# Feed-forward of a transformer pair: three of eight back products in half-precision terms, with the back products three steps behind

## The chip, the cores and the metric

The kernel runs on one core of one Trainium2 chip. The metric is the device time of one execution in microseconds. PE is the matrix engine (TensorE), DVE, ACT and POOL are VectorE, ScalarE and GpSimd; SP issues most transfers.

## What is computed

Two transformer layers on x of 4 x 1024 tokens of 256 values: cross-attention, a mixture of experts, a second cross-attention, and last a low-rank feed-forward, each on the normalised rows and added to x. The change is in the last one:

```
P = x_normalised @ U1            # 256 -> 64
H = gelu(P @ V1 + b1)            # 64 -> 1024, tanh form
Q = H @ U2                       # 1024 -> 64
x = x + Q @ V2 + b2              # 64 -> 256
```

All inputs and the output are single precision.

## The kernel before

Stages follow one another: preparation, first attention, routing, a stage that runs the experts and then the second attention (`experts_and_attend`), and `feed_forward` (from L2189). The feed-forward works in eight units of 512 tokens (UNITS). A unit's 1024 hidden values are eight steps m of 128 (MS); j counts steps over all units. Every engine has its own instruction list, written out by hand in loops, and the lists meet in semaphores.

The steps of a unit, with the names of the program:
- `unit_rows` (L2114) and `unit_normed` (L2131) on DVE and `unit_deviation` (L2124) on POOL normalise a row tile of 128 tokens: statistics (L2117, L2119), variance plus epsilon (L2121), the power -0.5 on POOL (L2128), and the normalised row (L2136). POOL also adds b2 to the row of x (`biased`, L2231). The same functions serve the first four row tiles at the end of the second attention.
- `rows_transposed` (L2249, four transposes into x_ps) on PE, copied out by ACT (L2315).
- `low_rank` (L2256): x times U1 into 64 rows for each half of the unit, one half on column half 0 to 63 of the array, the other on 64 to 127. ACT takes its high half in half precision (`high`, L2321), DVE the low rest (`low`, L2351).
- `first(u, m)` (L2269): six half-precision products on row halves of the array (three terms, two halves), into one of two banks h_ps.
- `gelu(u, m)` on ACT (L2327): h_ps to h in single precision, four buffers.
- `back(u, m)` (L2279): h times U2, single precision, two products on the two column halves, accumulated over m in low2_ps.
- `second` (L2356) copies low2_ps to SBUF, PE's `result` (L2288) multiplies by V2, DVE's `result` (L2364) adds x, SP stores.

On PE the order of a unit is first 0, first 1, the result of the unit before, then back m and first m + 2 in turn, the low rank of the next unit, and backs 6 and 7. A first waits until the gelu two steps earlier has read its bank; a back waits for its gelu. In the second attention DVE's `sums` and `heads` (L2024, L2031) feed PE's L1696; `expand` (L2042, L2044), which splits V1 into half-precision terms, stands in DVE's list there, in the step k = QUARTERS - 4.

```
for m in range(6):
    back(u, m)
    first(u, m + 2)
    if more and m in (1, 4):
        rows_transposed(2 * u + 2 + m // 4)
```

Of the kernel before, what the change touches and what calls it, by code (L numbers as in the profile page):

```python
# [31 lines left out]
P = 128  # L32
# [1254 lines left out]
def experts_and_attend(nc, A, G):  # L1287
# [3 lines left out]
    with ExitStack() as ctx:  # L1291
# [79 lines left out]
        with nc.Block() as block:  # L1371
# [538 lines left out]
            def _(dve):  # L1910
# [135 lines left out]

                for c in range(SOON, CHUNKS):
                    weights(c)
# [18 lines left out]
                for k in STEPS:  # L2067
# [22 lines left out]
                    if k == QUARTERS - 4:  # L2090
                        expand()
                    if QUARTERS - 3 <= k <= QUARTERS:
                        unit_rows(nc, dve, G, k - QUARTERS + 3)
# [20 lines left out]
def unit_rows(nc, dve, G, n):  # L2114
# [3 lines left out]
    dve.wait_ge(f.ch, 2 * n + 1)  # L2118
    nc.vector.bn_aggr(f.mv[:, i, :], f.stats[:, i, :]).then_inc(f.ch, 1)  # L2119
    dve.wait_ge(f.ch, 2 * n + 2)  # L2120
    nc.vector.tensor_scalar(f.ve[:, i, :], f.mv[:, i, 1:2], EPS, None, ALU.add).then_inc(f.var_ok, 1)  # L2121


def unit_deviation(nc, pool, G, n):  # L2124

    f = G["f"]
    pool.wait_ge(f.var_ok, n + 1)
    nc.gpsimd.tensor_tensor(f.rstd[:, n % 4, :], f.ve[:, n % 4, :], G["neghalf"][:, :], ALU.pow).then_inc(f.rstd_ok, 1)  # L2128


def unit_normed(nc, dve, G, n):  # L2131

    f = G["f"]
    dve.wait_ge(f.rstd_ok, n + 1)
# [28 lines left out]
def allocate_last(nc, ctx, G):  # L2163
# [15 lines left out]
    G["b1"], G["w2"], G["b2"] = Q.sb("b1_f", [P, HID // P]), Q.sb("v2_f", [2 * RANK, D]), Q.sb("b2_f", [P, D])  # L2179
    G["ff_in"] = L.sem("ff_in")  # L2180
# [8 lines left out]
def feed_forward(nc, A, G):  # L2189
# [3 lines left out]
    UNITS, U, MS = NT // 4, 4 * P, HID // P  # L2193
    with ExitStack() as ctx:
# [5 lines left out]
        h = Q.sb("h_f", [P, 4, U])  # L2200
# [7 lines left out]
        b2_ok = L.sem("b2_ok_f")  # L2208
# [4 lines left out]
        u1, w1, w1h, b1, u2, w2, b2 = (G[n] for n in ("u1", "w1", "w1h", "b1", "u2", "w2", "b2"))  # L2213

        with nc.Block() as block:  # L2215
# [24 lines left out]
            def _(pe):  # L2240
# [19 lines left out]
                def first(u, m):  # L2260
                    j = u * MS + m
                    if m == 0:
                        pe.wait_ge(llo_ok, u + 1)
                        if u == 0:
                            pe.wait_ge(w1h_ok, 2)
# [7 lines left out]
                def back(u, m):  # L2273
                    j = u * MS + m
                    pe.wait_ge(h_ok, j + 1)
                    if m == 0:
                        after(pe, low2_ok, u)
                    for i in range(2):
                        last = mm(low2_ps[flat(i, RANK), :], u2[:, m, :], h[:, j % 4, flat(i, U // 2)],  # L2279
                                  start=m == 0, stop=m == MS - 1)  # L2280
# [12 lines left out]
                for u in range(UNITS):  # L2293
                    more = u + 1 < UNITS
                    first(u, 0)
                    first(u, 1)
                    if u:
                        result(u - 1)
                    for m in range(6):
                        back(u, m)  # L2300
                        first(u, m + 2)
                        if more and m in (1, 4):
                            rows_transposed(2 * u + 2 + m // 4)
# [118 lines left out]
```

## Time and profile before

| | |
|---|---|
| median of 3 runs | 997.5 us (995.8 to 999.16) |
| the profiled execution | 1003.9 us |
| its span in the trace | 1001.9 us |
| PE busy | 918.6 us, 92% of the span |
| DVE, ACT, POOL busy | 616.3, 513.4, 422.1 us |
| TensorE clock granted, mean | 0.97 of full |

The span runs from the first to the last instruction of the trace; the profiled execution's time has 2.0 us more around it. Shares over the whole span mix stages with different limits, so a stage has to be read by itself: the feed-forward lies at the end, from about 903 us on.

### The profile page before, as it was taken

The numbers are of one execution on the slowest core, as the hardware profiler recorded it, in microseconds if no ns is written. First come the engines' busy times: TensorE is split into PE (matmuls) and PEld (weight loads), VectorE is DVE, ScalarE is ACT, GpSimd is POOL, SyncE is SP. The second block draws the span as 40 slices with busy tenths as digits, with TensorE's granted clock in tenths as the row PEclk, the third lists the DMA queues.
The fourth block names the chain that finished last, engine by engine and source line by source line (L and its number), as shares of the span: only waits on it lengthen the run. The fifth ranks groups of instructions, "written<-read, shape, count | busy, mean of one in ns | idle before, by whom it ended". The sixth has DMA issues, their size and how long they took to land. (4 is left out here: it accounts for less than half of the span.)

```text
span 1001.9 us, 23945 instructions
## 1 busy us (share of the span) xinstructions
PE 918.6 (92%) x8022; PEld 640.7 (64%) x8022; DVE 616.3 (62%) x1517; ACT 513.4 (51%) x873; POOL 422.1 (42%) x573
## 2 busy tenths in 40 slices
PE   6799999997458999999999999999989999889995
PEld 4555656554226788898898888888734444454552
DVE  3577888885787434454554545677468888545661
ACT  1478888886352433333333333333456767645663
POOL 2387777772201122334333224553176665204450
PEclk9999999999876999999999999999989999999998
DMA  6423444424541112111111212232143221000112
GB/s 178 89 65 106 114 145 117 141 88 151 154 160 43 44 44 59 43 43 54 54 43 48 60 44 67 90 90 68 33 113 91 81 78 39 2 1 15 51 46 61
DMA packets 73731, 75.46 MB, mean 75 GB/s; under 512 B 22730, under 2 KB 66874, under 8 KB 73626
## 3 DMA queue, kind: packets, MB, share of 16 engines
q1 hardware_dynamic: 67146, 56.31, 18.8%
q0 software_dynamic: 6480, 17.70, 6.7%
q8 instruction: 72, 1.18, 0.5%
q14 instruction: 33, 0.27, 0.1%
HBM read 51.64 MB, written 22.34 MB: 74 GB/s over the span
## 5 line engine op out<-in xcount | busy, mean ns | idle before, releaser
L1925 DVE CAST hh_e<-h_e 128x512 f16<-128x512 f32 x128 | 57.7, 451 | 151.6 <-ACT h_e L1800 87.7
L1564 PE MATMUL banks_ea<-xT_e,experts 128*128 128x256 f16 x512 | 139.6, 273 | 0.0
L1579 PE MATMUL banks_ea<-experts,hh_e 128*128 x512 | 139.6, 273 | 0.0
L1566 PE MATMUL banks_ea<-xT_e,experts 128*128 128x256 f16 x512 | 139.6, 273 | 0.0
L1580 PE MATMUL banks_ea<-experts,hh_e 128*128 x512 | 139.6, 273 | 0.0
L1565 PE MATMUL banks_ea<-xT_e,experts 128*128 128x256 f16 x512 | 139.6, 273 | 0.0
L1578 PE MATMUL banks_ea<-experts,hh_e 128*128 x512 | 139.6, 273 | 0.0
L1800 ACT ACTIVATE h_e<-banks_ea 128x512 f32<-128x512 f32 x128 | 76.4, 597 | 87.3 <-PE banks_ea L1566 87.3
L1383 POOL DMA_INDIRECT x_e<-xh_scratch,token x33 | 36.8, 1114 | 151.5 <-PE banks_ea L1505 105.5
L1927 DVE TENSOR_TENSOR hh_e<-h_e,hh_e 128x512 f16<-128x512 f32 x128 | 88.6, 692 | 4.4
L1854 ACT ACTIVATE experts<-banks_ea 77x1024 f32<-77x1024 f32 x64 | 64.8, 1014 | 41.0 <-PE banks_ea L1673 41.0
L625 POOL TENSOR_TENSOR experts<-keys,blocks 128x616 f16<-128x616 f16 x64 | 76.5, 1216 | 0.0
L1408 POOL DMA_INDIRECT w_late<-y_scratch,slots_t x64 | 62.5, 977 | 30.7 <-issue 16.7
L2010 DVE TENSOR_REDUCE lx<-banks_ea 128x4 f32<-128x308 f32 x128 | 60.3, 471 | 18.5 <-PE banks_ea L1644 18.0
L835 ACT ACTIVATE experts<-sT_ps 77x1024 f32<-77x1024 f32 x64 | 65.1, 1016 | 7.3 <-PE sT_ps L694 4.2
L1790 ACT ACTIVATE xT_e<-banks_ea 128x512 f16<-128x512 f32 (+1 forms) x39 | 21.8, 558 | 91.3 <-PE banks_ea L1505 91.3
L1380 POOL COPY idx_e<-token 128x2 int32 x19 | 11.6, 611 | 119.1 <-PE banks_ea L1505 119.1
L2327 ACT ACTIVATE experts<-h_ps_f,experts 128x512 f32<-128x512 f32 x64 | 43.2, 688 | 30.2 <-PE h_ps_f L2269 30.2
L928 DVE TENSOR_REDUCE qcat<-s_ps 128x8 f16<-128x616 f32 x64 | 51.0, 798 | 8.5 <-PE s_ps L720 4.3
L1817 ACT ACTIVATE y_e<-banks_ea 128x256 f32<-128x256 f32 x64 | 21.1, 381 | 67.0 <-PE banks_ea L1580 67.0
L1579 PEld LDWEIGHTS banks_ea<-experts,hh_e 128*128 128x128 f16 x512 | 50.0, 98 | 6.2
L1565 PEld LDWEIGHTS banks_ea<-xT_e,experts 128*128 x512 | 50.0, 98 | 6.2
(376 smaller groups left out, 2193.8 us busy)
## 6 DMA issues: line engine op xcount, KB each, us to landing
experts<-in_L_ffn_w SPq DMA_DIRECT2D x22, 512.0 KB, 4.0
y_scratch<-y_e SPq DMA_DIRECT2D x32, 256.0 KB, 3.3
x<-in_x SPq DMA_DIRECT2D x32, 128.0 KB, 3.2
experts<-in_x SPq DMA_DIRECT2D x64, 64.0 KB, 2.4
x_scratch<-x SPq DMA_DIRECT2D x16, 256.0 KB, 2.5
xh_scratch<-xn SPq DMA_DIRECT2D x16, 256.0 KB, 2.7
w_late<-in_L_ffn_w SPq DMA_DIRECT2D x8, 512.0 KB, 4.6
w_late<-x_scratch SPq DMA_DIRECT2D x32, 128.0 KB, 2.6
```

The lines of the kernel that those rows point to most:

```text
L625: nc.gpsimd.tensor_tensor(bd[:, f % 2, flat(i, 2), :, :], G["khi"][0][:, b, heads].rearrange("p (q k) -> p q k", q=2)[:, :, None, :] .broa ...
L835: nc.scalar.activation(prob[:, k % 2, qh, :, :], sT_ps[0:KEYS, :, :], ACT.Exp).then_inc(exp_ok, 1)
L1408: pool.indirect_dma_start(out=rows[:, f % 4, :], out_offset=None, in_=A["y"][0:EARLY_ROWS, :] if f < TB else A["y"], in_offset=bass.Indire ...
L1564: mm(out, w[0], xT[0][:, c, :], start=c == 0, stop=False)
L1565: mm(out, w[0], xT[1][:, c, :], start=False, stop=False)
L1566: last = mm(out, w[1], xT[0][:, c, :], start=False, stop=c == DC - 1)
L1578: mm(out, a[0], w[0], start=m == 0, stop=False)
L1579: mm(out, a[0], w[1], start=False, stop=False)
L1580: last = mm(out, a[1], w[0], start=False, stop=m == 7)
L1800: nc.scalar.activation(h[:, q % 2, :], up_ps[q], ACT.Gelu, scale=1 / WSCALE).then_inc(gelu_ok, 1)
L1854: nc.scalar.activation(prob[:, k % 2, 2 * half:2 * half + 2, :], sT_ps[0:KEYS, 2 * half:2 * half + 2, :], ACT.Exp, scale=1.0 / 16).then_in ...
L1927: nc.vector.tensor_tensor(hh[1][own], h[own], hh[0][own], ALU.subtract).then_inc(hlo_ok, 1)
```

## The change

In steps m = 1, 3 and 5 of every unit (SPLITS, 24 in all) the back product is made of half-precision terms. ACT runs the gelu a second time on the same bank, into half precision (hh, part 0). DVE subtracts it from the single-precision gelu (`split`, hh, part 1). U2 is multiplied by 64 and split in the same way into u2h (`expand_back`, after `expand`), and the back is three terms: high by high, high by low, low by high. The other five backs use the scaled U2 in single precision, and `second` divides by 64.

The backs trail the firsts by three steps (LAG) through all units without a break; the buffers of h become six (RING). The result of a unit moves behind first 3 of the next, low rank to step 6, the transposes to steps 2 and 4. DVE's list is rearranged, and its variance add (L2121) moves to POOL.

```diff
+                def expand_back():
+                    nc.vector.tensor_scalar(G["u2"][:, :, :], G["u2"][:, :, :], WSCALE, None, ALU.mult).then_inc(unit.w1h_ok, 1)
+                    dve.wait_ge(unit.w1h_ok, 3)
+                    nc.vector.tensor_copy(G["u2h"][:, 0, :, :], G["u2"][:, :, :]).then_inc(unit.w1h_ok, 1)
+                    dve.wait_ge(unit.w1h_ok, 4)
+                    nc.vector.tensor_tensor(G["u2h"][:, 1, :, :], G["u2"][:, :, :], G["u2h"][:, 0, :, :],
+                                            ALU.subtract).then_inc(unit.w1h_ok, 1)
...
                     if k == QUARTERS - 4:
                         expand()
+                        expand_back()
...
     nc.vector.bn_stats(f.stats[:, i, :], G["X"](n)).then_inc(f.ch, 1)
-    dve.wait_ge(f.ch, 2 * n + 1)
-    nc.vector.bn_aggr(f.mv[:, i, :], f.stats[:, i, :]).then_inc(f.ch, 1)
-    dve.wait_ge(f.ch, 2 * n + 2)
-    nc.vector.tensor_scalar(f.ve[:, i, :], f.mv[:, i, 1:2], EPS, None, ALU.add).then_inc(f.var_ok, 1)
+    dve.wait_ge(f.ch, n + 1)
+    nc.vector.bn_aggr(f.mv[:, i, :], f.stats[:, i, :]).then_inc(f.var_ok, 1)
...
     pool.wait_ge(f.var_ok, n + 1)
+    nc.gpsimd.tensor_scalar(f.ve[:, n % 4, :], f.mv[:, n % 4, 1:2], EPS, None, ALU.add).then_inc(f.rstd_ok, 1)
+    pool.wait_ge(f.rstd_ok, 2 * n + 1)
     nc.gpsimd.tensor_tensor(f.rstd[:, n % 4, :], f.ve[:, n % 4, :], G["neghalf"][:, :], ALU.pow).then_inc(f.rstd_ok, 1)
...
-    UNITS, U, MS = NT // 4, 4 * P, HID // P
+    UNITS, U, MS, RING, LAG = NT // 4, 4 * P, HID // P, 6, 3
+    SPLITS = [(u, m) for u in range(UNITS) for m in (1, 3, 5)]
...
-        h = Q.sb("h_f", [P, 4, U])
+        h, hh = Q.sb("h_f", [P, RING, U]), Q.sb("hh_f", [P, 4, 2, U], F16)
...
-                            pe.wait_ge(w1h_ok, 2)
+                            pe.wait_ge(w1h_ok, 5)
                     after(pe, h_ok, j - 1)
...
                 def back(u, m):
                     j = u * MS + m
-                    pe.wait_ge(h_ok, j + 1)
                     if m == 0:
                         after(pe, low2_ok, u)
-                    for i in range(2):
-                        last = mm(low2_ps[flat(i, RANK), :], u2[:, m, :], h[:, j % 4, flat(i, U // 2)],
-                                  start=m == 0, stop=m == MS - 1)
+                    if (u, m) in SPLITS:
+                        n = SPLITS.index((u, m))
+                        pe.wait_ge(split_ok, n + 1)
+                        for weight, part in ((0, 0), (0, 1), (1, 0)):
+                            for i in range(2):
+                                last = mm(low2_ps[flat(i, RANK), :], u2h[:, weight, m, :], hh[:, n % 4, part, flat(i, U // 2)],
+                                          start=m == weight == part == 0, stop=m == MS - 1 and weight == 1)
+                    else:
+                        pe.wait_ge(h_ok, j + 1)
+                        for i in range(2):
+                            last = mm(low2_ps[flat(i, RANK), :], u2[:, m, :], h[:, j % RING, flat(i, U // 2)],
+                                      start=m == 0, stop=m == MS - 1)
                     last.then_inc(back_done, 1)
...
                 low_rank(0)
-                for u in range(UNITS):
-                    more = u + 1 < UNITS
-                    first(u, 0)
-                    first(u, 1)
-                    if u:
+                for j in range(UNITS * MS + LAG):
+                    u, m = j // MS, j % MS
+                    if u < UNITS:
+                        first(u, m)
+                    if u and m == LAG and u < UNITS:
                         result(u - 1)
-                    for m in range(6):
-                        back(u, m)
-                        first(u, m + 2)
-                        if more and m in (1, 4):
-                            rows_transposed(2 * u + 2 + m // 4)
-                    if more:
+                    if u + 1 < UNITS and m == 6:
                         low_rank(u + 1)
-                    back(u, 6)
-                    back(u, 7)
+                    if j >= LAG:
+                        back((j - LAG) // MS, (j - LAG) % MS)
+                    if u + 1 < UNITS and m in (2, 4):
+                        rows_transposed(2 * u + 1 + m // 2)
                 result(UNITS - 1)
...
                 def gelu(u, m):
                     j = u * MS + m
                     act.wait_ge(h_done, j + 1)
-                    after(act, back_done, j - 3)
-                    nc.scalar.activation(h[:, j % 4, :].rearrange("p (i t) -> p i t", i=2), h_ps[j % 2], ACT.Gelu_apprx_tanh,
-                                         bias=b1[:, m:m + 1], scale=1 / WSCALE).then_inc(h_ok, 1)
+                    after(act, back_done, j - RING + 1)
+                    first = nc.scalar.activation(h[:, j % RING, :].rearrange("p (i t) -> p i t", i=2), h_ps[j % 2],
+                                                 ACT.Gelu_apprx_tanh, bias=b1[:, m:m + 1], scale=1 / WSCALE)
+                    if (u, m) not in SPLITS:
+                        first.then_inc(h_ok, 1)
+                        return
+                    n = SPLITS.index((u, m))
+                    if n >= 4:
+                        before = SPLITS[n - 4]
+                        act.wait_ge(back_done, before[0] * MS + before[1] + 1)
+                    nc.scalar.activation(hh[:, n % 4, 0, :].rearrange("p (i t) -> p i t", i=2), h_ps[j % 2],
+                                         ACT.Gelu_apprx_tanh, bias=b1[:, m:m + 1], scale=1 / WSCALE).then_inc(h_ok, 1)
 
                 high(0)
                 for u in range(UNITS):
                     more = u + 1 < UNITS
                     for m in range(MS):
                         gelu(u, m)
-                        if more and m in (3, 6):
-                            rows(2 * u + 2 + m // 6)
-                    if more:
-                        high(u + 1)
+                        if more and m in (2, 4):
+                            rows(2 * u + 1 + m // 2)
+                        if more and m == 6:
+                            high(u + 1)
...
-                    nc.vector.tensor_copy(low2[:, :], low2_ps).then_inc(low2_ok, 1)
+                    nc.vector.tensor_scalar(low2[:, :], low2_ps, 1 / WSCALE, None, ALU.mult).then_inc(low2_ok, 1)
+
+                def split(u, m):
+                    j = u * MS + m
+                    n = SPLITS.index((u, m))
+                    dve.wait_ge(h_ok, j + 1)
+                    if n >= 4:
+                        before = SPLITS[n - 4]
+                        dve.wait_ge(back_done, before[0] * MS + before[1] + 1)
+                    nc.vector.tensor_tensor(hh[:, n % 4, 1, :], h[:, j % RING, :], hh[:, n % 4, 0, :],
+                                            ALU.subtract).then_inc(split_ok, 1)
...
+                def next_row(n):
+                    if n < NT:
+                        if n + 1 < NT:
+                            rows(n + 1)
+                        normed_rows(n)
+
                 rows(4)
                 low(0)
+                next_row(4)
+                next_row(5)
                 for u in range(UNITS):
+                    if u == 0:
+                        next_row(6)
+                    next_row(4 * u + 7)
+                    if u:
+                        second(u - 1)
+                    split(u, 1)
+                    if u:
+                        result(u - 1)
+                    next_row(4 * u + 8)
+                    split(u, 3)
+                    next_row(4 * u + 9)
+                    split(u, 5)
                     if u + 1 < UNITS:
-                        for n in range(4 * u + 4, 4 * u + 8):
-                            if n + 1 < NT:
-                                rows(n + 1)
-                            normed_rows(n)
-                            if u and n % 4 == 2:
-                                result(u - 1)
                         low(u + 1)
-                    elif u:
-                        result(u - 1)
-                    second(u)
+                    next_row(4 * u + 10)
+                second(UNITS - 1)
                 result(UNITS - 1)
```

The order on PE around the border of two units, before. x_ps with 64x256 is the low rank, with 128x128 the transposes; h_ps is the first product, low_ps the back product, out_ps the result.

```order
L2269 MATMUL h_ps_f<-experts 128x256 x6
L2256 MATMUL x_ps_f<-experts 64x256 x4
L2279 MATMUL low_ps_f<-experts 64x256 x4
L2269 MATMUL h_ps_f<-experts 128x256 x12
L2288 MATMUL out_ps_f<-experts 128x256 x4
L2279 MATMUL low_ps_f<-experts 64x256 x2
```

The same border in the changed kernel, from the back product of step 3 to the result; L2294 is a split back, L2299 one in single precision.

```order
L2294 MATMUL low_ps_f<-experts 64x256 x6
L2281 MATMUL h_ps_f<-experts 128x256 x6
L2299 MATMUL low_ps_f<-experts 64x256 x2
L2281 MATMUL h_ps_f<-experts 128x256 x6
L2294 MATMUL low_ps_f<-experts 64x256 x6
L2281 MATMUL h_ps_f<-experts 128x256 x6
L2299 MATMUL low_ps_f<-experts 64x256 x2
L2281 MATMUL h_ps_f<-experts 128x256 x6
L2299 MATMUL low_ps_f<-experts 64x256 x2
L2261 MATMUL x_ps_f<-const,experts 128x128 x4
L2281 MATMUL h_ps_f<-experts 128x256 x6
L2308 MATMUL out_ps_f<-experts 128x256 x4
```

Two firsts or two backs no longer stand side by side, and three backs of a unit come after firsts of the next.

DVE's list at the end of the second attention, before:

```order
L2037 TENSOR_TENSOR experts<-banks_ea,experts 128x256
L2042 TENSOR_SCALAR experts<-experts 128x1024
L2044 SCALAR_TENSOR_TENSOR experts<-experts 128x1024
L2024 RECIPROCAL experts<-banks_ea 128x16
L2031 TENSOR_TENSOR experts<-banks_ea,experts 128x256
```

and in the changed kernel:

```order
L2037 TENSOR_TENSOR experts<-banks_ea,experts 128x256
L2042 TENSOR_SCALAR experts<-experts 128x1024
L2044 SCALAR_TENSOR_TENSOR experts<-experts 128x1024
L2049 TENSOR_SCALAR experts<-experts 128x512
L2051 CAST experts<-experts 128x512
L2053 TENSOR_TENSOR experts<-experts 128x512
L2024 RECIPROCAL experts<-banks_ea 128x16
L2031 TENSOR_TENSOR experts<-banks_ea,experts 128x256
```

The three instructions of `expand_back` stand ahead of the `sums` and `heads` of the same step.

DVE's list in unit 0, from the normalised row 6 on, before (L2351 is the low half of unit 1):

```order
L2136 TENSOR_SCALAR experts<-const,experts 128x256
L2117 BN_STATS experts<-experts 128x6
L2119 BN_AGGR experts<-experts 128x2
L2121 TENSOR_SCALAR experts<-experts 128x1
L2136 TENSOR_SCALAR experts<-const,experts 128x256
L2351 TENSOR_TENSOR experts<-x_ps_f,experts 128x256
```

and in the changed kernel (L2391 is `split`):

```order
L2146 TENSOR_SCALAR experts<-const,experts 128x256
L2127 BN_STATS experts<-experts 128x6
L2129 BN_AGGR experts<-experts 128x2
L2146 TENSOR_SCALAR experts<-const,experts 128x256
L2391 TENSOR_TENSOR experts<-experts 128x512
```

The first split stands behind row 7, and the low half of unit 1 behind the third split.

## Rows read from the trace of the kernel before

**Rows 1.** Stretches: length; busy of PE, PEld (weight loads), DVE, ACT, POOL; clock; DMA.

```profile
940.00:952.00 12.00, 11.92 (x120) 5.96 (x116) 7.42 (x25) 7.45 (x12) 6.30 (x11) 1.00 0.17 48
```

**Rows 2.** Timeline of PE, one unit: start, length, engine, line, operation.

```profile
937.59 0.83 PE L2269 MATMUL h_ps_f<-experts 64*128 64x256 f16 x12
938.25 1.03 PE L2288 MATMUL out_ps_f<-experts 64*128 64x256 f32 x8
939.21 0.65 PE L2279 MATMUL low_ps_f<-experts 128*64 128x256 f32 x4
939.79 0.50 PE L2269 MATMUL h_ps_f<-experts 64*128 64x256 f16 x6
940.23 0.65 PE L2279 MATMUL low_ps_f<-experts 128*64 128x256 f32 x4
...
947.40 1.03 PE L2279 MATMUL low_ps_f<-experts 128*64 128x256 f32 x8
948.51 0.83 PE L2269 MATMUL h_ps_f<-experts 64*128 64x256 f16 x12
```

**Rows 3.** Timeline, end of the second attention; in brackets idle time and its releaser.

```profile
873.59 1.22 DVE L2044 SCALAR_TENSOR_TENSOR experts<-experts 128x1024 f16<-128x1024 f32 x1
...
875.49 0.44 PE L1696 MATMUL banks_ea<-const,experts 128*128 128x128 f32 x2 [1.38 <-DVE experts L2031]
...
876.84 2.06 PE L1704 MATMUL banks_ea<-woT,experts 128*128 128x256 f32 x4
```

**Rows 4.** Timelines of PE and its weight loads: experts, and one feed-forward load.

```profile
500.06 0.27 PE L1566 MATMUL banks_ea<-xT_e,experts 128*128 128x256 f16 x1
500.17 0.27 PE L1578 MATMUL banks_ea<-experts,hh_e 128*128 x1
...
500.17 0.10 PEld L1579 LDWEIGHTS banks_ea<-experts,hh_e 128*128 128x128 f16 x1
...
936.90 0.14 PEld L2279 LDWEIGHTS low_ps_f<-experts 128*64 128x64 f32 x2
```

**Rows 5.** Timeline of PE in the first attention: half-precision products of three shapes.

```profile
203.07 0.28 PE L703 MATMUL t_ps<-ident,experts 128*128 128x128 f16 x2
203.27 0.33 PE L715 MATMUL s_ps<-experts 64*32 64x308 f16 x8
203.53 0.30 PE L720 MATMUL s_ps<-late,early 5*128 5x308 bf16 x2
```

**Rows 6.** Groups by line: busy us, mean ns of one, idle us before.

```profile
L2327 ACT ACTIVATE experts<-h_ps_f,experts 128x512 f32<-128x512 f32 x64 | 43.2, 688 | 30.2 <-PE h_ps_f L2269 30.2
...
L1927 DVE TENSOR_TENSOR hh_e<-h_e,hh_e 128x512 f16<-128x512 f32 x128 | 88.6, 692 | 4.4
...
L1925 DVE CAST hh_e<-h_e 128x512 f16<-128x512 f32 x128 | 57.7, 451 | 151.6 <-ACT h_e L1800 87.7 <-PE banks_ea L1580 59.9 <-PE banks_ea L1545 3.8
...
L2136 DVE TENSOR_SCALAR experts<-experts 128x256 f32<-128x256 f32 x24 | 12.3, 513 | 0.0
...
L2121 DVE TENSOR_SCALAR experts<-experts 128x1 f32<-128x1 f32 x32 | 4.9, 154 | 1.1
...
L2128 POOL TENSOR_TENSOR experts<-experts,neghalf 128x1 f32<-128x1 f32 x32 | 20.0, 625 | 77.0 <-DVE experts L2121 77.0
...
L2231 POOL TENSOR_TENSOR experts<-experts 128x256 f32<-128x256 f32 x24 | 17.3, 724 | 0.0
...
L639 POOL TENSOR_SCALAR ve<-mv 128x1 f32<-128x1 f32 x32 | 7.7, 240 | 39.5 <-DVE mv L922 39.5
```

**Rows 7.** Timeline of PE, the first products of units 0 and 1.

```profile
905.14 0.83 PE L2269 MATMUL h_ps_f<-experts 64*128 64x256 f16 x12 [0.94 <-DVE experts L2351]
...
915.73 0.83 PE L2269 MATMUL h_ps_f<-experts 64*128 64x256 f16 x12
```

**Rows 8.** Timeline of PE, the last back product.

```profile
989.88 0.65 PE L2279 MATMUL low_ps_f<-experts 128*64 128x256 f32 x4 [0.20 <-ACT experts L2327]
```

**Rows 9.** Table of stretches for PE: busy us, instructions, clock, DMA share, GB/s.

```profile
878.00:880.00 2.00, 2.00 (x11) 0.50 0.00 0
```

More of the change, by code:

```diff
@@ L2133, in unit_normed @@
     f = G["f"]
-    dve.wait_ge(f.rstd_ok, n + 1)
+    dve.wait_ge(f.rstd_ok, 2 * n + 2)
     after(dve, f.t_done, (n - 4) // 2 + 1)
@@ L2179, in allocate_last @@
     G["b1"], G["w2"], G["b2"] = Q.sb("b1_f", [P, HID // P]), Q.sb("v2_f", [2 * RANK, D]), Q.sb("b2_f", [P, D])
+    G["u2h"] = Q.sb("u2h_f", [P, 2, HID // P, RANK], F16)
     G["ff_in"] = L.sem("ff_in")
@@ L2207, in feed_forward @@
         xh_ok, t_done, xhT_ok, w1h_ok = f.xh_ok, f.t_done, f.xhT_ok, f.w1h_ok
-        b2_ok = L.sem("b2_ok_f")
+        b2_ok, split_ok = L.sem("b2_ok_f"), L.sem("split_ok_f")
         low_done, lhi_ok, llo_ok, h_done, h_ok, back_done, low2_ok, out_done, out_ok = (
@@ L2212, in feed_forward @@
         ident = G["const"][:, CC["ident"][0]:CC["ident"][1]]
-        u1, w1, w1h, b1, u2, w2, b2 = (G[n] for n in ("u1", "w1", "w1h", "b1", "u2", "w2", "b2"))
+        u1, w1, w1h, b1, u2, u2h, w2, b2 = (G[n] for n in ("u1", "w1", "w1h", "b1", "u2", "u2h", "w2", "b2"))
         with nc.Block() as block:
```

## Prediction

> **What bounds the kernel now.** I read the table of stretches first: in the middle of the feed-forward PE is busy 11.92 of 12.00 us, ACT 7.45, DVE 7.42, POOL 6.30 [rows 1]. PE sets the pace there and the others have a third to spare. The timeline of PE then shows one unit of 512 tokens [rows 2]: from the pair of first products at 937.59 to the next such pair at 948.51 is 10.92 us, each row starts before the one ahead of it ends, and none carries a wait. From start to start a back product takes 0.58 (939.21 to 939.79), a first product 0.44 (939.79 to 940.23), two adjacent firsts 0.66, the last two backs 1.11 with a short wait for the low halves in it. A unit changes by what these times add up to.
>
> The end of the attention, where the change adds three DVE instructions, is another matter. There PE waited 1.38 us for DVE's L2031 at 875.49, right after the expansion of the first weights (L2044 at 873.59) [rows 3]. What DVE gets to do at that place is paid in full.
>
> **Part 1: the split backs.** In 24 backs (three of eight in each of eight units) two single-precision products become six half-precision ones, on the same two column halves of the array. No row has half precision in this tile shape, so I bound it.
> - Streaming: in the expert stage a half-precision product of 256 columns starts every 0.11 us (500.06, 500.17) [rows 4]. Three pairs side by side are 0.33, which is also half of the 0.66 of two firsts.
> - Are the column halves side by side? In the first attention eight half-precision products of 308 columns, on 64 rows by 32 columns each, go from 203.27 to 203.53 [rows 5]. One by one, at the rate above, they would take 1.06, in row pairs alone 0.53. Column tiles run together in half precision.
> - The change of tile shape: a first costs 0.33 where the result product follows (half of 0.66) and 0.44 where a back follows. The result is single precision like the back, so the 0.10 belongs to the shape and not to the type. From half-precision transposes on 128 rows (two of 128 columns, 0.11 of streaming) to products on 64 rows it took 0.20 (203.07 to 203.27) [rows 5]: 0.09 again. If the eight products above all ran at once, 0.13 of their 0.26 was streaming and 0.13 overhead.
> - Weight loads: six instead of four. Two single-precision loads for the column halves lay within 0.14 at 936.90, and in the experts a load of 0.10 stands beside every product of 0.11 on the same rows [rows 4]. So I count none. The Trainium skill, "TensorE: Matmul & The Clock Gate", Part 3, The mechanism, states that a weight load overlaps products in flight only when the row groups differ. The halves share all rows; by that rule three pairs of loads of 0.10 would stand alone, a split would take 0.73, and the sum below would be +7.7 instead of +0.5. The expert products would then be 0.21 apart, and the trace has 0.11.
>
> I take 0.33 + 0.10 = 0.43 against 0.58: 0.15 saved in each. The ends are 0.33 (the shape costs nothing) and 0.46 (an overhead of 0.13).
>
> **Part 2: the new order on PE.** Result, low rank and transposes stay as many. Before, a unit held 0.66 (two firsts) + 6 x 0.58 + 6 x 0.44 + 1.11 = 7.89. Now firsts and backs alternate all the way: seven firsts at 0.44, one at 0.33 ahead of the result, five backs at 0.58, three splits at 0.43: 3.08 + 0.33 + 2.90 + 1.29 = 7.60. That is 0.29 less a unit. Some 0.2 of what the splits save is given back, because firsts and backs no longer stand in pairs. Units 1 to 6 give **-1.8 us**.
>
> **Part 3: cover on ACT, DVE and POOL.** The shares of rows 1 are, for one unit of 10.92, ACT 6.8, DVE 6.8, POOL 5.7. ACT gets three gelus at 0.69: 8.9. DVE gets three subtracts of 128x512, 0.69 by the same form in the experts, and loses four adds of 0.15: 8.2. POOL gets four adds of 0.24: 6.7 [rows 6]. All stay below the 10.6 of PE, so they cost nothing there. A split is ready some 2 us after its first product, its back comes three steps, 3 to 4 us, after it. The tightest place is the low half for the next unit, which stands behind the third subtract on DVE and ahead of the next unit's first product, with about 0.2 us of room; what it is late would be paid in seven units.
>
> **Part 4: unit 0.** It lasted 10.59 us (905.14 to 915.73) [rows 7]. Three backs slide into the next unit (-1.74), two of its own are split (-0.30). Against that, DVE now normalises rows 4 to 7 ahead of the first subtract, and POOL paces them: add 0.24, power 0.62, bias 0.72, so 1.58 a row [rows 6]. From some 0.5 us after the first product it needs 0.86 for row 5 and 2 x 1.58 for rows 6 and 7; with row 7 itself (0.51) and the subtract (0.69) the second back can start near 5.7. PE is there near 4.1 and stands 1.6 us. The third first product and the first transposes wait some 0.6 longer than PE waited here before. -2.04 + 2.2 = **+0.2**.
>
> **Part 5: the last unit.** It also does three backs of the unit before, 0.43 + 2 x 0.58 = 1.59. It saves 3 x 0.15 in its own splits, its last back no longer waits 0.20 for the last gelu [rows 8], and its last four backs stand together, two changes of shape less (0.2). **+0.8.**
>
> **Part 6: the end of the attention.** Scaling, cast and subtract of the second weights, 128x512 each, are 0.45 + 0.45 + 0.69 = 1.59 by the casts and subtracts of the experts [rows 6], and they stand between L2044 and the L2031 that PE waits for. Nothing hides them. Of the four adds of the variance (0.15 each) that leave DVE here I count two: the first falls where PE is busy, and for the last row DVE waits for POOL, which now does the add. **+1.3**. The ends: 0, if the steps after it take it up, and 2.3 by the clock. After the old wait the granted clock was 0.50 (878 to 880) [rows 9], the 1.2 GHz level, and L1704 took 2.06 at 876.84 [rows 3], half of which would do at full clock. A longer wait could bring one more such piece, 1.0 us, into the slow stretch.
>
> **Sum.** -1.8 + 0.2 + 0.8 + 1.3 = **+0.5 us**. The profiled execution took 1003.9 (span 1001.9, 2.0 around it) and would come to 1004.4. It lies 6.4 above the median of three runs, 997.5, so on that median the forecast is **998.0**. A measurement of this kernel tells about 0.3%, 3 us, from no change: I forecast no change.
>
> **Rivals.**
> - *The halves do not stream together* (slower). Six products in a line, 0.65 + 0.10 = 0.75 a split: 24 x 0.32 = +7.7 more, time 1005.7. For it: no half precision in just this shape. Against: rows 5. It decides from a split of 0.53 on, where the sum passes +3. Chance 0.05.
> - *Weight loads stand alone* (slower). 24 x 0.30 = +7.2, time 1005.2. For it: all six products of a split use all 128 rows. Against: both loads of rows 4. Chance 0.04.
> - *The shape costs nothing between half-precision products* (faster). First and split 0.33 each: 24 x 0.20 = -4.8, time 993.2. Against: the 0.20 of rows 5, with half precision on both sides. Chance 0.08.
> - *The clock falls once more*, in unit 0 where PE stands, or for longer in the attention. A slow stretch like that of rows 9 costs 1.0 to 1.7: time 999.0 to 999.7, beyond 3 us only with another miss. Chance 0.12.
> - *The change does not do what it says, because ACT or DVE takes over.* They would have to lose 2 us a unit to waits; one us beyond that is +7, time 1005. Against: part 3. Chance 0.05.
>
> The forecast has the rest, 0.66, spread over 994 to 1002 by the ends of part 1 (24 x 0.03 = 0.7 up), those of part 6, and the spread of runs (995.8 to 999.16); 0.08 of it lies beyond 3 us on either side. Faster: 0.08 + 0.08 = 0.16. Slower: 0.05 + 0.04 + 0.05 + 0.08, and 0.04 from the clock, 0.26. The same: 0.58. The range goes from the cheap shape (993.2, nearly) to the clock at its worst with the spread of runs: 993.5 to 1002.0.
>
> **What would show it.** Right: six products of a split in 0.42 to 0.46 from start to start, units of 10.6 us without a wait on PE, one wait of 1 to 2 us for DVE's subtract in unit 0, and a wait for L2031 near 2.9 instead of 1.38. Wrong: a split of 0.53 or more (part 1), firsts that wait for gelus or low halves in steady units (part 3), a wait for L2031 as before (part 6), or a granted clock of 0.50 within the feed-forward.

## The result, and the profile after

| | before | after |
|---|---|---|
| median | 997.53 us (994.53 to 1003.49) | 1000.7 us (998.14 to 1020.47) |
| ratio of the times | | 1.0033, 95% interval 1.0016 to 1.0049 |
| profiled execution, its span | 1003.9, 1001.9 | 1005.88, 1004.1 |
| PE, DVE, ACT, POOL busy | 918.6, 616.3, 513.4, 422.1 | 916.7, 631.9, 526.3, 434.1 |

The medians are of 20 runs each; the run of 1020.47 us, at a granted clock of 0.92, is left out of the ratio, as single runs far off are below. The changed kernel is 3.3 us slower (1.6 to 4.9). The forecast was no change, +0.5 us; the time lies within its range. Both profiled executions lie above their medians. Both also ran some 7 us at the lower clock from about 737 us on, ahead of everything that the change touches (granted clock 0.62 and 0.53 from 736 to 744 before, 0.56 and 0.59 after); in the profiles of other executions, further down, this stretch is there or not.

The steady units of the feed-forward did what they were meant to. The table of stretches of the changed kernel, columns as in [rows 1], shows PE busy without a gap; DVE and ACT have grown, and stay below PE:

```profile
940.00:952.00 12.00, 12.00 (x130) 6.18 (x126) 9.25 (x23) 9.30 (x16) 7.98 (x15) 1.00 0.20 55
```

PE's timeline of one unit, which answers to [rows 2]; L2281 is a first product, L2294 a split back, L2299 a back in single precision, L2308 the result:

```profile
943.53 1.03 PE L2308 MATMUL out_ps_f<-experts 64*128 64x256 f32 x8
944.49 0.65 PE L2299 MATMUL low_ps_f<-experts 128*64 128x256 f32 x4
945.07 0.50 PE L2281 MATMUL h_ps_f<-experts 64*128 64x256 f16 x6
945.51 0.52 PE L2294 MATMUL low_ps_f<-experts 128*64 128x256 f16 x6
945.96 0.66 PE L2261 MATMUL x_ps_f<-const,experts 128*128 128x128 f32 x4
...
954.19 1.03 PE L2308 MATMUL out_ps_f<-experts 64*128 64x256 f32 x8
```

The split back takes 0.45 from start to start (945.51 to 945.96), the single one 0.58 (944.49 to 945.07), and no row carries a wait. The next result starts at 954.19, so a unit lasts 10.66 instead of 10.92.

At the end of the attention DVE, and PE behind it (both in the timeline, for [rows 3]):

```profile
873.07 1.23 DVE L2044 SCALAR_TENSOR_TENSOR experts<-experts 128x1024 f16<-128x1024 f32 x1
...
874.21 0.42 DVE L2049 TENSOR_SCALAR experts<-experts 128x512 f32<-128x512 f32 x1
874.67 0.43 DVE L2051 CAST experts<-experts 128x512 f16<-128x512 f32 x1
875.13 0.69 DVE L2053 TENSOR_TENSOR experts<-experts 128x512 f16<-128x512 f32 x1
875.74 0.25 DVE L2024 RECIPROCAL experts<-banks_ea 128x16 f32<-128x16 f32 x1
876.02 0.42 DVE L2031 TENSOR_TENSOR experts<-banks_ea,experts 128x256 f32<-128x256 f32 x1
...
876.50 0.69 PE L1696 MATMUL banks_ea<-const,experts 128*128 128x128 f32 x2 [2.91 <-DVE experts L2031]
...
878.96 2.08 PE L1704 MATMUL banks_ea<-woT,experts 128*128 128x256 f32 x4
...
883.49 0.44 PE L1696 MATMUL banks_ea<-const,experts 128*128 128x128 f32 x2
```

PE's wait for L2031 grew from 1.38 to 2.91. The next round, from L1696 to L1696, took 6.99 (876.50 to 883.49); before it took 5.47 (875.49 to 880.96). The stretches say why: the clock stays at its lower level (0.50, 1.2 GHz) for about twice as long as before (PE first, then PEld, DVE, ACT, POOL, clock). The changed kernel:

```profile
876.00:878.00 2.00, 1.50 (x10) 0.45 (x10) 0.42 (x1) 0.38 (x1) 0.00 (x0) 0.60 0.00 0
878.00:880.00 2.00, 2.00 (x11) 0.86 (x4) 0.00 (x0) 0.91 (x2) 0.00 (x0) 0.50 0.00 0
880.00:882.00 2.00, 2.00 (x11) 1.38 (x13) 0.90 (x4) 0.60 (x1) 0.00 (x0) 0.50 0.00 0
882.00:884.00 2.00, 2.00 (x22) 0.75 (x22) 0.61 (x3) 0.40 (x1) 0.81 (x2) 0.69 0.00 0
```

and the kernel before, on either side of the stretch of [rows 9], with the start of its next round:

```profile
876.00:878.00 2.00, 2.00 (x11) 0.98 (x4) 0.00 (x0) 1.37 (x3) 0.00 (x0) 0.72 0.00 0
...
880.00:882.00 2.00, 2.00 (x26) 0.65 (x18) 0.70 (x3) 0.93 (x2) 0.55 (x1) 0.92 0.00 0
...
880.96 0.44 PE L1696 MATMUL banks_ea<-const,experts 128*128 128x128 f32 x2
```

I count the clock lost there as the sum of (1 - clock) x 2 us over such rows: 3.4 us; before, with 0.72, 0.50 and 0.92 from 876 to 882, 1.7. A stretch at the lower clock that loses 1.7 us is called a patch in what follows.

Unit 0, for [rows 7], with its waits and the first product of unit 1 (918.37); the first product of the last unit (982.33) and its end, for [rows 8]:

```profile
907.35 0.83 PE L2281 MATMUL h_ps_f<-experts 64*128 64x256 f16 x12 [0.94 <-DVE experts L2377]
908.63 0.50 PE L2281 MATMUL h_ps_f<-experts 64*128 64x256 f16 x6 [0.46 <-ACT experts L2344]
909.78 0.66 PE L2261 MATMUL x_ps_f<-const,experts 128*128 128x128 f32 x4 [0.64 <-DVE experts L2146]
...
913.53 0.52 PE L2294 MATMUL low_ps_f<-experts 128*64 128x256 f16 x6 [1.64 <-DVE experts L2391]
...
918.37 0.50 PE L2281 MATMUL h_ps_f<-experts 64*128 64x256 f16 x6
...
982.33 0.50 PE L2281 MATMUL h_ps_f<-experts 64*128 64x256 f16 x6
...
991.52 1.03 PE L2299 MATMUL low_ps_f<-experts 128*64 128x256 f32 x8
993.08 1.13 PE L2308 MATMUL out_ps_f<-experts 64*128 64x256 f32 x8 [0.53 <-DVE experts L2382]
```

The last unit in the kernel before:

```profile
981.29 0.83 PE L2269 MATMUL h_ps_f<-experts 64*128 64x256 f16 x12
...
991.06 1.13 PE L2288 MATMUL out_ps_f<-experts 64*128 64x256 f32 x8 [0.53 <-DVE experts L2356]
```

The groups by line that answer to [rows 6] (the subtract, the normalised row, POOL's add and power) and to the loads of [rows 4]:

```profile
L2391 DVE TENSOR_TENSOR experts<-experts 128x512 f16<-128x512 f32 x24 | 16.9, 704 | 3.2 <-ACT experts L2353 3.2
L2146 DVE TENSOR_SCALAR experts<-experts 128x256 f32<-128x256 f32 x24 | 14.9, 619 | 1.8 <-POOL experts L2138 1.8
L2136 POOL TENSOR_SCALAR experts<-experts 128x1 f32<-128x1 f32 x32 | 9.0, 282 | 61.9 <-DVE experts L2129 61.9
L2138 POOL TENSOR_TENSOR experts<-experts,neghalf 128x1 f32<-128x1 f32 x32 | 22.0, 688 | 2.7
L2294 PEld LDWEIGHTS low_ps_f<-experts 128*64 128x64 f16 x144 | 6.7, 109 | 6.5 <-issue 3.2 <-DVE experts L2391 1.9
```

The sum, term by term, from the two profiles:

| term | forecast | measured | from |
|---|---|---|---|
| units 1 to 6 | -1.8 | -1.60 | first of unit 1 to first of unit 7: 63.96 (918.37 to 982.33), before 65.56 (915.73 to 981.29) |
| unit 0 | +0.2 | +0.43 | 11.02 (907.35 to 918.37), before 10.59 |
| last unit | +0.8 | +0.98 | its first product to the last result: 10.75 (982.33 to 993.08), before 9.77 (981.29 to 991.06) |
| end of attention | +1.3 | +2.73 | wait +1.53; next round +1.52; the three rounds behind it -0.22, -0.21, +0.11 |
| sum | +0.5 | +2.5 | |

So the feed-forward gives -0.2 instead of -0.8, and the end of the attention costs twice what was forecast.

### The profile page after: what moved, and what is told of

It is laid out like the page before. It is cut to its first block and busy times, and to the rows that moved or that the text cites. A ratio compares the mean times of both kernels' runs of the same rounds, so it can differ in the third digit from the quotient of the medians.

```text
span 1004.1 us, 24110 instructions
## 1 busy us (share of the span) xinstructions
PE 916.7 (91%) x8070; PEld 640.6 (64%) x8070; DVE 631.9 (63%) x1512; ACT 526.3 (52%) x897; POOL 434.1 (43%) x605
## 5 line engine op out<-in xcount | busy, mean ns | idle before, releaser
L1565 PEld LDWEIGHTS banks_ea<-xT_e,experts 128*128 x512 | 50.1, 98 | 6.1
L1566 PEld LDWEIGHTS banks_ea<-xT_e,experts 128*128 x512 | 50.1, 98 | 5.8
```

Source lines behind the costliest of these rows:

```text
L1565: mm(out, w[0], xT[1][:, c, :], start=False, stop=False)
L1566: last = mm(out, w[1], xT[0][:, c, :], start=False, stop=c == DC - 1)
```

## The experiments

Theory 1: the loss is made at the end of the attention, by DVE's three instructions ahead of L2031 and what follows from them; the feed-forward gives about nothing. Theory 2, the rival: the loss is made in the feed-forward (second gelus, subtracts, POOL), and the stretch at the attention's end is a matter of one execution. Within theory 1 it is open whether the slow clock comes of the longer pause (1b) or differs by chance from execution to execution (1a, "a matter of the throw").

**back_in_gap and both_in_gap.** In each step of the attention PE works on the scores while DVE waits. The second expansion, then both, go to that place, ahead of DVE's `result(n)`:

```diff
+                    if k == QUARTERS - 4:
+                        expand()
+                    if k == QUARTERS - 3:
+                        expand_back()
                     if tile(n):
                         result(n)
...
-                    if k == QUARTERS - 4:
-                        expand()
-                        expand_back()
```

back_in_gap moves `expand_back` alone. Expected:

> The changed kernel, with the three instructions for the second weights moved behind the heads of the next step, where DVE waits 2.5 us for PE anyway. If the loss is made at the attention's end (a wait longer by 1.5, and a slow clock after it), PE's wait for L2031 is back to 1.3 to 1.5 us, the stretch from the last L1673 of that step to the first product of the feed-forward is 2.7 us shorter than in the changed kernel (34.2 to 31.5), and the time is 0 to 0.5 us below the kernel before. If the loss is made in the feed-forward and the profile only shows one throw of the clock, the time stays 2 us or more above before.

> The changed kernel with both expansions in DVE's gaps, one a step. By the first theory PE has no wait over 0.3 us for L2031 in that step, the clock stays at 1.00 there, the stretch is 4 to 5 us shorter than in the changed kernel, and the time is 1.5 to 2.5 us below before. By the second the time stays above before.

Measured: 997.18 us, ratio to the kernel before 0.9997 (0.9971 to 1.0022), and 996.22, 0.9983 (0.9963 to 1.0004). The loss is gone with the place of the three instructions, and the program of the feed-forward is unchanged. By the times alone this is not decided: the interval of back_in_gap overlaps that of the changed kernel a little, and both_in_gap was expected 1.5 to 2.5 below the kernel before and is 1.7 below by the ratio, with an interval that takes in 1. The profiles decide it: PE's wait is back at 1.38 in back_in_gap, and from the last L1673 of that step to the first product of the feed-forward it is 31.2 us instead of 34.2 (expected 31.5):

```profile
867.65 0.44 PE L1696 MATMUL banks_ea<-const,experts 128*128 128x128 f32 x2 [1.38 <-DVE experts L2031]
```

The first wait for L2031 of both_in_gap, and the next, which the statistics and normalised rows of DVE cause:

```profile
876.54 0.44 PE L1696 MATMUL banks_ea<-const,experts 128*128 128x128 f32 x2 [0.27 <-DVE experts L2031]
881.01 0.44 PE L1696 MATMUL banks_ea<-const,experts 128*128 128x128 f32 x2 [1.55 <-DVE experts L2031]
```

**before_and_back.** The other way round: the kernel before with `expand_back` and nothing else of the change (`second` divides by 64; the half-precision copies of U2 are not used).

```diff
                     if k == QUARTERS - 4:
                         expand()
+                        expand_back()
```

> The kernel before with the expansion of the second weights alone, at the changed kernel's place, and the division by 64; its half-precision copies are not used. By the first theory 1.5 us (the wait) to 3.0 us (with the clock) above before, with units of 10.93 in the feed-forward. By the second 0 to 1.3 us above.

Measured: 999.8 us, ratio 1.0023 (0.9993 to 1.0052), so some two thirds of the loss, though the interval takes in 1. The wait is the changed kernel's to the hundredth:

```profile
870.01 0.44 PE L1696 MATMUL banks_ea<-const,experts 128*128 128x128 f32 x2 [2.91 <-DVE experts L2031]
```

**fillers and fillers_in_wait.** 24 products whose result nobody reads keep PE at work, in the changed kernel. In the first run they stood one step early, where PE had no wait (`k == QUARTERS - 4`); in the second right ahead of the products that wait for L2031.

```diff
+                    if k == QUARTERS - 3:
+                        pe.wait_ge(max_ok, 4 * NT)
+                        for i in range(24):
+                            mm(s_ps[:, 0:D], G["ident16"][:, :], G["khi"][1][:, 0, 0:D], start=True, stop=True)
                     if tile(n):
                         heads_transposed(n)
```

> The changed kernel with 24 products into an unused bank while PE waits for L2031 (they leave the wait as long as it is). If the slow clock follows from the longer pause, the granted clock stays at 1.00 behind it, the next round of that loop takes 5.0 instead of 6.99 us, and the time falls by 1.5 to 2.0 us against the changed kernel, to about 1 us above before. If the slow stretch comes by chance of phase, as often before as after, the median falls no more than the one of the kernel before would, and the ratio to before stays near 1.003.

> The changed kernel with 24 extra half-precision products, into a bank whose content is not needed, in PE's list right ahead of the products that wait for L2031, one step later than in the run before this one; the result of the kernel is the same. Theory 1b (the longer pause, 2.91 us, brings the slow clock that makes the next round 6.99 instead of 5.47): PE works through the pause, the granted clock stays at 1.00 behind it, and the time is 1 to 2 us below the changed kernel: 999 us. Theory 1a (the wait itself is the whole loss, the clock there is a matter of the throw): the time is that of the changed kernel, 1000.7, or a little above it, and the round behind the wait is still long in the profile. In both the first product after the wait starts when L2031 ends, so the wait's own 1.5 us stay.

Measured: 1003.39 us, ratio 1.006 (1.0035 to 1.0086), with the fillers' own time on PE (2.6 in their round); the time was expected to fall and rose, so it says nothing of the clock. In the profile, behind a pause of 2.81 the clock stayed at 1.00, and the round took 4.15 (871.91 to 876.06). That execution was one of the fastest of its twelve (998.43 us, clock 0.980 over the whole run); in nine of the other eleven the clock over the whole run was 0.965 to 0.973, so its profile is not typical of them:

```profile
871.91 0.44 PE L1696 MATMUL banks_ea<-const,experts 128*128 128x128 f32 x2 [2.81 <-DVE experts L2035]
876.06 0.44 PE L1696 MATMUL banks_ea<-const,experts 128*128 128x128 f32 x2
```

With the fillers in the pause: 999.7, ratio 1.0027 (1.0001 to 1.0053). The first product behind L2031 came no sooner (7.11 after the round's start, as in the changed kernel), the next round took 4.15, but two rounds later, behind a wait of 1.56, the clock fell after all:

```profile
870.16 0.44 PE L1696 MATMUL banks_ea<-const,experts 128*128 128x128 f32 x2 [0.18 <-DVE experts L2035]
874.31 0.44 PE L1696 MATMUL banks_ea<-const,experts 128*128 128x128 f32 x2
...
883.33 0.44 PE L1696 MATMUL banks_ea<-const,experts 128*128 128x128 f32 x2 [1.56 <-DVE experts L2035]
```

The ratio does not separate 1a from 1b. What it shows is that filling one pause doesn't shorten the wait itself, and that the slow patch can come at a later one.

**all_in_gaps, before_in_gaps, gaps_no_splits.** All that DVE does for the feed-forward at the attention's end goes into the gaps, one step earlier. POOL's addition of b2 runs eight row tiles behind instead of four, which takes it out of unit 0:

```diff
+                    if k == QUARTERS - 5:
+                        expand()
+                    if k == QUARTERS - 4:
+                        expand_back()
+                    if QUARTERS - 4 <= k < QUARTERS:
+                        unit_rows(nc, dve, G, k - QUARTERS + 4)
+                    if QUARTERS - 3 <= k <= QUARTERS:
+                        unit_normed(nc, dve, G, k - QUARTERS + 3)
                     if tile(n):
                         result(n)
...
-                    biased(n - 4)
-                for n in range(NT - 4, NT):
+                    if n >= 8:
+                        biased(n - 8)
+                for n in range(NT - 8, NT):
```

before_in_gaps makes the same moves in the kernel before (without `expand_back` and without the later addition of b2). gaps_no_splits is all_in_gaps with `SPLITS = []`: all backs are computed in single precision, in the new order.

> The changed kernel with every DVE instruction for the feed-forward at the end of the attention (both expansions, the statistics and the normalised rows of the first four row tiles) moved into the part of the step in which PE works and DVE waits, and POOL's addition of the bias eight row tiles behind instead of four, so that POOL's adds and powers of unit 0 are not queued behind it. Theory 1 (the loss is made at the attention's end): the waits for L2031 of 2.91, 1.6 and 1.4 us shrink to some 0.3 each, and the time is 2 to 4 us below the kernel with both expansions moved (996.2): 993 us. Unit 0 goes from 11.02 to about 10 us by POOL's part. Theory 2 (the loss is made in the feed-forward): no more than the 1 us of unit 0 is gained, 995 us or more.

> The kernel before with its own expansion, statistics and normalised rows moved into the same places at the attention's end; nothing else changed. Control for the run above: what is gained here belongs to the attention's end alone and not to the half-precision backs or their order. Theory 1: the wait of 1.38 and those of the two steps after it shrink to some 0.3, 2 to 3.5 us below the kernel before: 994 us. If the time stays at 997, the waits there are not what bounds the stretch (POOL or the banks are next).

> The kernel with everything moved (the run all_in_gaps) with all eight backs of every unit in single precision: no second gelu, no subtract, no half-precision products; the new order stays. It prices the split: by rows 0.58 against 0.445, 24 x 0.135 = 3.2 us, so the time is 3.2 us above all_in_gaps, and a unit lasts 11.05 instead of 10.66. If the second gelus and the subtracts cost something that hides in the unit (theory 2), the difference is smaller, down to nothing.

Measured, beside the same runs of the kernel before: all_in_gaps 990.29 us, ratio 0.9917 (0.9893 to 0.9942); before_in_gaps 992.21, 0.9931 (0.9908 to 0.9954); gaps_no_splits 993.52, 0.9952 (0.9928 to 0.9976). all_in_gaps beats the kernel before by 8 us, and the changed kernel by more. Some 6 of the 8 are the attention's end and lie in the kernel before as well (before_in_gaps is 6.9 below it by the ratio, and its stretch A, defined below, 5.4 shorter). Both times are lower than was expected; the waits for L2031 are gone but for the one of the last step, and two waits of unit 0 have shrunk from 0.64 and 1.64, so that unit 0 lasts 9.54 instead of 11.02 (forecast 10):

```profile
885.07 0.44 PE L1696 MATMUL banks_ea<-const,experts 128*128 128x128 f32 x2 [0.81 <-DVE experts L2031]
...
900.29 0.66 PE L2262 MATMUL x_ps_f<-const,experts 128*128 128x128 f32 x4 [0.26 <-DVE experts L2146]
...
902.94 0.52 PE L2295 MATMUL low_ps_f<-experts 128*64 128x256 f16 x6 [0.55 <-DVE experts L2392]
```

The splits alone are worth 3.2 us by the medians (993.52 - 990.29; the intervals of the two ratios overlap) and 2.4 by the profiles' feed-forward (86.61 - 84.25). A unit without them lasts 11.04, with them 10.66, in the kernel before 10.93: the splits save 0.38 a unit and the order costs 0.11. Theory 2 falls for the steady units: three splits at 0.13 to 0.15 saved each make the 0.38, so the second gelus and the subtracts cost PE next to nothing there.

**after_again, after_third, before_again, before_third.** Both kernels unchanged, for more profiles of the disputed round.

> The changed kernel once more, unchanged, for a second profile and a second comparison: how long is the round behind the wait for L2031 of 2.91 us? Theory 1b (the longer pause regularly brings a doubly long slow clock): 6.8 to 7.0 us from L1696 to L1696 again, against 4.15 at full clock and 5.4 with one slow piece; the time is 3 us above the kernel before. Theory 1a (the clock there is a matter of the throw): any of 4.15, 5.4 and 7.0, and the mean loss beyond the wait's own 1.5 us is not to be laid on this place.

> The changed kernel a third time, for its profile alone. As the run before: 1b expects 6.8 to 7.0 us again, 1a any of 4.15, 5.4 and 7.0.

> The kernel before once more, for its profile: the round behind the wait of 1.38 us lasted 5.47 with one slow piece. 1b: 5.4 again, since the pause is the same. 1a: 4.15 or 5.4.

> The kernel before a third time, for its profile. As the run before: 1b expects 5.4 again, 1a 4.15 or 5.4.

Measured: after_again 1002.92 us, ratio 1.0044 (1.0019 to 1.0068), the loss once more. The single executions: 998.56 (after_third), 1001.46 (before_again), 997.53 (before_third). The round behind the wait took 6.93, 5.46, 5.47 and 4.36; the second and the last are not what 1b expected. In after_third the second slow patch came later, still ahead of the feed-forward; its stretches:

```profile
870.00:872.00 2.00, 2.00 (x11) 1.17 (x4) 0.00 (x0) 1.37 (x3) 0.00 (x0) 0.66 0.00 0
872.00:874.00 2.00, 2.00 (x14) 1.17 (x16) 1.19 (x5) 0.27 (x1) 0.19 (x1) 0.50 0.00 0
...
890.00:892.00 2.00, 1.94 (x9) 1.58 (x10) 0.86 (x4) 1.97 (x4) 0.00 (x0) 0.78 0.00 0
892.00:894.00 2.00, 2.00 (x8) 1.77 (x7) 0.74 (x3) 0.95 (x3) 0.00 (x0) 0.50 0.00 0
894.00:896.00 2.00, 2.00 (x12) 1.49 (x10) 0.42 (x1) 0.85 (x2) 0.00 (x0) 0.87 0.00 0
```

Put together: A is the time from the L1696 of the round that ends in the expansion's wait to the first product of the feed-forward, F from there to the last result product, "lost" the clock lost within A.

| profile | waits for L2031 | lost | A | F |
|---|---|---|---|---|
| before, three profiles | 1.38, 0 to 0.16, 0.5 to 0.6, 1.76, 1.31 | 1.7, 1.7, 0 | 35.23, 35.22, 34.01 | 85.92, 85.93, 85.92 |
| after, three profiles | 2.91, 0, 0.37, 1.55, 1.42 | 3.4, 3.4, 3.4 | 37.96, 37.89, 37.84 | 85.73, 85.74, 85.73 |
| before_and_back | 2.91, 0, 0.58, 1.76, 1.31 | 1.7 | 36.70 | 85.93 |
| back_in_gap | 1.38, 0, 0.34, 1.56, 1.42 | 1.7 | 34.98 | 87.29 |
| both_in_gap | 0, 0, 0.27, 1.55, 1.42 | 0 | 32.13 | 85.73 |
| fillers | 2.81, 0, 0.34, 1.55, 1.43 | 0 | 34.93 | 85.73 |
| fillers_in_wait | 0.18, 0, 0.35, 1.56, 0.28 | 1.7 | 35.62 | 85.74 |
| all_in_gaps | 0, 0, 0, 0.81, 0 | 0 | 29.38 | 84.25 |
| before_in_gaps | 0, 0, 0, 0.81, 0 | 0 | 29.38 | 85.92 |
| gaps_no_splits | 0, 0, 0, 0.81, 0 | 0 | 29.38 | 86.61 |

On the mean of three profiles each the change makes A longer by 3.1 (37.90 against 34.82) and F shorter by 0.19: +2.9, which is the measured +3.3 and +4.4 within their intervals. Of the 3.1, 1.2 is waits at equal clock (1.53 less 0.32 for the adds). The rest, 1.9, goes with the slow clock: 3.4 us lost in every profile of after, 1.1 on the mean in those of before. In the profiles, theory 1 stands.

Between 1a and 1b: with the long pause the profiles lost 3.4 three times, 1.7 once (before_and_back), and nothing once (fillers, where PE had the extra work in the round ahead of the pause). With waits of 1.3 to 1.8 and no longer one they lost 1.7 in four and nothing in two (before_third, both_in_gap). Without a wait above 0.81 nothing was lost in three. So the slow clock goes with the pauses, but neither every time nor at a fixed place; three profiles with pauses lost nothing either, so it isn't shown that the pauses bring it. The changed kernel lost two patches in three of three profiles, the kernel before in none; but before_and_back has the same pause and one patch.

The clock listed for every run says more of this than the profiles. Span x (1 - clock), the clock lost over a whole run wherever it fell, is on the mean 24.7 us in the kernel before (83 runs, standard error 0.4) and 28.8 in the changed kernel (31 runs, 0.6). So the change does bring slow clock, 4.0 more on the mean. But it is 25.6 (12 runs, 1.2) in before_and_back, which has the long pause, and 27.9 (12 runs, 1.3) in fillers_in_wait, where PE works through it. The pause alone doesn't account for the loss, and 1b is not borne out; what brings the slow clock stays open. back_in_gap and both_in_gap have 26.0 and 26.3 (0.9 and 0.6), which is more than the kernel before although their waits for L2031 are together no longer than there. Part of it may therefore lie outside the attention's end, behind the wait of 1.64 in unit 0 as in the profile of back_in_gap, and to that extent theory 2 is not ruled out.

## Why the prediction was right, and where it failed

- **Part 1 (splits) was right.** 0.43 taken, 0.43 to 0.46 measured, within its ends of 0.33 and 0.46; the one split that is followed by another back, at 991.19, takes 0.33, so the 0.10 is the change of shape. The first two rivals fell (a split of 0.53 or more never shows), as did the cheap shape. The rule of the Trainium skill, "TensorE: Matmul & The Clock Gate", Part 3, The mechanism, would have made it 0.73; the six loads of 109 ns in each split of 0.45 have to lie beside products on the same rows.
- **Part 2 (order) was right:** 0.29 less a unit forecast, 0.26 measured; 0.16 forecast as given back by the alternation (of some 0.2), 0.11 measured with gaps_no_splits. Its 6 x 0.29 is 1.74 and stands there as 1.8, and the terms of Part 5 add up to 0.74, not 0.8; the two cancel in the sum.
- **Part 3 (cover) was right.** No steady unit waits; the tight place for the low half held in all seven units.
- **Part 4 (unit 0): the mechanism was right.** A row takes 1.58 on POOL from add to add (909.54 to 911.12), as forecast, and the split's wait is 1.64 (1.6). The sum was 0.2 short; that is likely what a unit gives back by alternating, an estimate from Part 2, which Part 4 had left out. **Part 5** was 0.2 short as well, for a cause that no run singles out.
- **Part 6 (end of the attention) is the step that failed, by its size.** "Nothing hides them", 1.59 for the three instructions and 0.30 for the adds were right: +1.53 and -0.32. What was mis-sized is the clock. I kept "one more such piece, 1.0 us" as an end of the range and took the clock as unchanged; all three profiles of the changed kernel lose one patch more than the worst of before, worth 1.5 in the first of them (6.99 against 5.47). Against the mean of the three profiles before the clock costs 1.9. The rival *the clock falls once more* had a chance of 0.12 and a price of 1.0 to 1.7; the price for one patch was about right, the chance was not, and it was not in the sum. What brings the second patch is open: the runs show that the pause alone doesn't account for it. [rows 3] and [rows 9] had the fact that mattered: PE stood 1.38 and the next round ran in part at half clock. A pause with slow clock behind it, made twice as long, should not have been priced at its length alone.
- With +2.7 in place of +1.3, and 0.6 lost in the feed-forward's small terms, the sum is +2.5, just below the 3 us that I called the bound of no change. The measured +3.3 lies on that bound; its interval doesn't decide between "the same" and "slower", but it excludes zero and the +0.5 of the sum. That 1000.7 lies in the range is owed to the upper end, which had the clock at its worst and the spread of runs in it, and not to the sum.

## What to carry to other kernels

Price a new instruction on a helper engine by where in its list it stands: the same three instructions cost about 3 us ahead of what PE waits for and next to nothing in a gap beside it, where DVE idles while PE works. A wait of PE that is followed by a stretch at the lower clock is dearer than its length, and a change that makes it longer may cost more than the added time: take several profiles of both kernels before laying a price on it, since the clock differs from execution to execution. And when a change shows such a place, look what else stands there: the expansions and normalised rows of the old kernel cost it some 6 us.

## What was not expected of the hardware

DVE's normalised row takes 0.41 alone and 0.80 where POOL's 128x256 addition (the b2 of `biased`) has begun just before. Timelines of DVE and POOL, the changed kernel in unit 0:

```profile
908.84 0.73 POOL L2243 TENSOR_TENSOR X_soon<-X_soon,experts 128x256 f32<-128x256 f32 x1
908.92 0.80 DVE L2146 TENSOR_SCALAR experts<-X_soon,experts 128x256 f32<-128x256 f32 x1 [0.21 <-POOL experts L2138]
```

and all_in_gaps, where the addition is gone from there:

```profile
899.82 0.41 DVE L2146 TENSOR_SCALAR experts<-X_soon,experts 128x256 f32<-128x256 f32 x1 [0.21 <-POOL experts L2138]
```

The first ends 0.15 behind POOL's (909.72 and 909.57). The Trainium skill, "SBUF — State Buffer", Who interferes with whom, states that DVE in a two-port mode and POOL take a shared pair of ports in turn, whoever issues first, and the other blocks until it is done. The order and the delay agree; a full block would end it 0.41 behind POOL's, and the trace has 0.15. With the addition moved, the feed-forward is 1.5 us shorter (F 85.73 to 84.25), all of it in unit 0. How much of that is the ports is not shown: the move also takes the addition's 0.73 out of POOL's list, which paced the rows.

The slow clock shows elsewhere in the feed-forward too: in back_in_gap it fell behind the 1.64 of unit 0 (F 87.29, 1.6 more), in the other profiles with that wait it did not.
